# Thirteen small zero stores in place of two large ones, and new orders for four engines

## The chip, the cores and the metric

The kernel runs on one core of one Trainium2 chip. The metric is device time in microseconds (us). The kernel before takes 718.44 us, the median of three runs (717.93 to 718.69). Inside the core, TensorE (PE) multiplies matrices, VectorE (DVE), ScalarE (ACT) and GpSimd (POOL) work element by element, and SyncE (SP) issues most of the DMAs, one queue in order. The engines meet at semaphores.

## The reference, cut to what matters

A context of 16 batches of 1601 keys meets 64 queries a batch (width 256, 16 heads of 16), then the 64 rows attend to themselves, then each row goes to one of eight experts that has room for 128 rows.

```python
x = x + xattn(layernorm(x), ctx, ctx, Wq, bq, Wk, bk, Wv, bv, Wo, bo)   # x: 16 x 64 x 256, ctx: 16 x 1601 x 256
x = x + self_attn_with_rope(layernorm(x), Wqkv, bqkv, Wout, bout)
x = x + moe(layernorm(x), wg, W, b)

# moe: T = 1024 rows, E = 8 experts, C = 128 places each
idx = argmax(softmax(xt @ wg)); mask = one_hot(idx, E)
locations = cumsum(mask, axis=0) - mask
mask = mask * (locations < C)
exp_in  = einsum('tec,th->ech', dispatch, xt)
exp_out = einsum('ech,efh->ecf', exp_in, W) + b[:, None, :]
out     = einsum('tec,ecf->tf', gate * dispatch, exp_out)
```

## The kernel before, in words

**Cross attention, by batch.** A batch b passes through four kinds of work on PE. `project` (letter K in the order, L807 and L816) makes keys and values in float32 quality from three bf16 products. The units 0 to 7 of a batch are its keys, in two halves of four; 8 to 14 are its values. ACT rounds the result of each (`khigh`, L1213), DVE keeps the rest (`klow`, L1481). SP then copies the key rows of a half to `kstack`, 12 DMAs of 100 KB (`keys(b)`, L501), three for each pair of heads. `max_scores` (m, L839) multiplies queries with these keys to find each row's maximum, which DVE reduces (`maxes`, L1498). `score_half` (s, L867) makes scores again with the maximum taken off, ACT takes the exponent (`prob`, L1235), and POOL makes its low part (`plow`, L637; in part of the last batch DVE, L1468). `weigh` (w, L891) multiplies with the values.

**The second part** follows from letter Z on, in eight tiles of 128 rows: output projection, layer norm, self attention, routing, experts. For the first five tiles the rows are scattered to slots in DRAM (`slot_x`, L703), read back by expert (L534), multiplied, written to `slot_y` (L539) and gathered (L711). The last three tiles go through all experts (letter F). A row without a place lands in a spare slot, so the slots of `slot_x` and the spare slots of `slot_y` must hold zeros first.

**The zeros.** POOL clears `zeros` (L555, 128 rows of 256 floats), which is the last tile of `att_all`. DVE overwrites that tile only in `attended(14)` and `attended(15)`. SP sends the zeros to DRAM behind the DMAs of `keys(4)` (L516, L518), 1024 KB and 640 KB. POOL waits for both before the first scatter (L700).

**What sets the order.** Each engine runs a list of letters written out by hand: `PE_PROGRAM`, `ACT_PROGRAM`, `DVE_PROGRAM`, `POOL_PROGRAM`. A letter calls the next piece of its kind. SP has no such list: its loop runs `send_queries(0)` and then `keys(b)` for each batch. `keys(b)` waits until batch b-2 has been scored, reads the queries from DRAM (`qstack`, L494), copies the keys half by half as DVE finishes them, in even batches sends the next queries (L485), and waits until batch b is projected before it loads the context of batch b+2 (`cbuf`, L507, 1601 KB). All of this is one queue: a DMA issued later moves behind those before it.

In the lists of the second part, A is `attention_columns`, H `norm_columns`, J `queries_keys`, V `values`; on DVE p is `low_prob`, N `normalised`, L `first_low`, a `attended`, k `query_moments`, z `query_variance`, B `weight_parts(1)`, j `query_rows`; on POOL c is `low_context`, f `fold`, v `first_values_low`, q `query_norm`, r `inverse_root`, t `second_constant`, Z `rooms_empty`, b `first_constant`, I `low_experts`; on ACT g is `query_high`.

Of the kernel before, what the change touches and what calls it, by code (L numbers as in the profile page):

```python
# [107 lines left out]


PE_PROGRAM = [  # L110
    ("KKKKKKKKKKKKKmmKmmKmmKKmmKmKmKmmKmKmKmKmmKmKmmKmKmKmmKmKmmKmmsKmssmKsmmsKmsmswwsmswmKswsmmswwwKmswwm"
     "smsKKsmwKmsmswwmswswmwsmswmwwsmsmKmmsswwmwmKmwswwswwsKsmsKwwsmsKmsmsKsmmwswwmswmswmKmsswwmsKmmswKmsm"
     "wKmsmwwswmKwsmsmwKmwmKmswmsKmwssmwwKmKmwwsKswKwmssmKsmwsmsKsmwwwKmwwsmsmwswwmKmssmKmsmKmmswswmswmsKm"
     "smwwwswmmswKmsKmswsmwmKmsmsKwwwKwwsmwKsswKwsmKmsmsKmssKmwsKwwsmwmwKswwsmswmsKmwmKmswmKsmsmwwsKmsswmK"
     "wmwmswswmsmwwKmswmsKmmKmswmKwwmKwswsKwsKssKmmsKmsswwmKsswmmwKswwsmmswwsKmswsmwmKsmwwsmsmwmsKsmmKmwsw"
     "wmmsKwsmwswsmwKmmKmKmmwwwKwswmwKssKssKsmKmssmKwmwwsmwwmsKsmKwwsmwmKsmmKmmswKswwmssKmsmwwwsmsKmsmwKsw"
     "mmswsKmwmwssmKmmKmKwswwwwmwKwssKssmmKsmsmKwswsmmsKwmswsmKwmwwmswsKwssmmwKsmmKwsmswmwswwswmsmKwsmKmwm"
     "swKmsmKwmKmwKwswmmwKmsKssKmswmsKsmswmKssmwmwwsmwKsmKwswsmmwsKwmKswmsmKmswwswmwKmsswwmKsmsKwmwsswmmww"
     "KmsmKmmsKmmwwwwKswmwKssKssKswsmwmKmsswwmmKsmwKwmsswmwsKmsmswwmwmKsmsmKmswsmwmswKswmmswKsmKmmsKmswwms"
     "mwKmmKwwwwswmwKssKswsmmKsmwswsmwwmsKsmmsKmwmsswwKmswmKwswKsmmswKsswmwmwKmmKmsKwsmwsmwsmKswmKmwmKmmsK"  # L120
     "msKwwswwwmKssKswwsKmsmwKmssmwwmswwmswsmKmsKmwwwssmwmKmmsKssKmmwKmwsmwsmwsmKswmswmKmmssKmmKmwswmwswws"
     "KwwmwKssKwsswmmKsKmswswwsmwwsmsmKmswswwmKmwssKKKwwmssmwwsmKmmssmKwwwmmKsmswwmwssKmmsKmsmKmwmKmmwwwww"
     "swmKKssKKsmsmKssmmwswwsKsmKswwwmssmKmmwswwmwmwsKwmmsKsmmsKmwwsmwmsKmmssKmmKmwwmssmKmswwmwswwwKswmKsw"
     "wsKssKsmsmKsmsKmmwwsKwwsKmsmwwwmswmswsmKmwsmswmwwKsmKssmKwwmwsmwwmKmmssKsmmsKmwKwsmwmwKmmKwsmKsmswmw"
     "wsmsmKmsmKsKsmwmwswswwwsmmsKmKwmswsmwwmmssKmsmKsmwmwssmwwmswwsmmKsmswmswwsmmZmwswAswwwswsAwsOssOswws"
     "swwswswsswwsswwwssHwsHswwswwVssJswwswswTAJOTSVwwwwSPPwwHWVJP2APTOoWSAH2OJoPhPVTHlWVJS2AToOhSPPlhWlPA"
     "2POcHWoJ2AVOHToJHSVhThJllTcPVSPSWPP2Wo2PPoxhWlxgchxgxl2gogFcFhFFFFlFFcFFFF", 1),
]
ACT_PROGRAM = [
    ("KgKKKKKKKKKKKKKKKgKKKKKKKKKKKKKRRKeKeeeeKeeeKeeKeeKeKeeeKeeeeeeeKeeeKRReeKeKeeeeKeeeKeeKeeKeeKKeeege"  # L130
     "KKeeKeeKeReKRKKeeKeeeeKeKeeeKeeKeKeeeKeeKeeKeeeKeKReeKKReKeKeeKeeeKeKeKeKeeKeeKeKeeeKeeeegeeKeKKeRKR"
     "KeKeeeKKeeKeeKeeeeKeeeKeeeKeeKKeeeeeKeKKKRKeRKeeKeeeKKeeKeeeKKeKKeeeeKeeKeeegKeeeKeKeRKKeRKeeeKeeKee"
     "eKeeKeKeeKeeKeeeeKeeKKeeKKKKReeKReeKeKeeeKeeKeeeeKeeKKeeKeKeeKeeegKeeKeKeKRKReKeeeKeKeeKeeKeeKeeKeee"
     "eKeeKeeKKeeKeKeeKRKReKeeKeeeeeeKKeeKeeKeKeeKeeKKeKeegeKeKKeReKKeReKeeKeeeKeeKeeeKKeeKeeeKKeeKeeKeeKe"
     "KeKReKeReKeeKeeKeeeeKeeeKeKeKKeeeKeeeKKeegeeKKeeKKRKReKeeKeKeeeKeeKeeeeKeKKeeeKeKeeKeeKKeeKReeRKeeKe"
     "eKeKeeKeKeKeeeKeeeKeKeeKeeKeKeeKeKeKKReKReKeeeKeeKeeeeKeKeeeKeeKeeKeeZeeeeKeeRReAeeeeAeeeeeeeeeeeeee"
     "HeeeeHeeeTAVBTBVEEPPHVEEA2PTPBAH2EEPfPHBViTV2ABTEEfPPfEiEiAPlP2H2AHVBTHVffBiiETElTBPVPEEPP2EE2PPxfhi"
     "xyxflhyxi2lyyfhil", 1),
]
DVE_PROGRAM = [  # L140
    ("jKKkKKzCKKkBzKKmmkmmzkmmKmmjmmKmKmmKKKmmmKmmKmKmmKmKmKmmKmKmKmmKmmKmmmmKmmKmKKmmmmmmKmmmmmKmmmKvKmKm"
     "mammKmmmKmmKmmKmmmKmjmmKKmmmKmmmKmKmKKKKmmmvmKmKmmmmKmmKmKmmmmmmmKmKmmzmKmKmmKaKKKKmmmKmvKmKmmmkKmmm"
     "KKmmammKmmKmmjmmKmKmmmKKmKKKvKzmKmmmKmmKmmKmmKmmmmmKmKmmmKmmmKkamKmmKmKKKvKmKKmmmKmmmKmmmmKaKmmmKmmK"
     "mjmmKzmmmKmmKmKmKKvKmmKmmKmKmmmKKmammmKmKmmmKmmmKmmKmmKKmmKKmKKmmKmmvKmmKmmmmKmKmKmmaKmmKmjmmKmKmmmK"
     "mmKmKKKvKmKmmKmkmmKmamKmmKmmmmmKmKmmKmKmmzmKmmKmmKKKvmKmmmmKmmKmKmKmmmKmmKmmKmmKjmmKmamKmmKmKmKKKKvm"
     "mKmmmmKmmmKmKmKmmKmmKmmmmKammKmKmmmKmKKKKmvmKmmKmammKKmmKmmmKmmmKKmmjmmKmKmmmKmmKmKKKKmvmKmmaKKmmmmm"
     "KmKmmmKmmKmmmKmmKmmKmmmKKmKKKvmKmmKKmmmKmmKmmmKmmmKmKmmKmmKmmKmmKKmmmKaKmmKmmvmKmKmmamKmKmmmmmKmKmmm"
     "mmKmmmmKmZpvXDGXDGppNNpLapTLppTXDGMMUUMNULvMUWTXDxGdWgNMnLUXMUDxGTNdaLgWTnMMUxUdXgDMnMUUWG1NX3LDWxGN"
     "dTXDLGgxNdngLTnMMUUT13MMUUMWUMUWxdgnxdqg1nqWq31qxdgyn3yyyfyy1ffyy3yyffyy", 1),
]  # L150
POOL_PROGRAM = [
    ("qqvvcfcccvvffvvcccfcvfppppppcppppppppppppppcpccpppppcqppppcpppcppcppppccppppppcpqpppcpppcpppppppcppc"
     "pcpppppppcpcpqpcpppcpppccpppppcppppppcpccpppppppcpppppcppqpcpppppcppccpppppcppppcppppccpppppcpppppcp"
     "pcpqcpppppppppppcppppcccppppcpppppccpppcppppppcpcppppcpppcppppppppppppppppbbppprrpppZbbttbtbrrRIbrbR"
     "IRrtrtstsrRRIIsssttRYRYRgYgggg", 1),
]


# [1682 lines left out]
```

## Time and profile before

| what | value |
|---|---|
| three runs | 717.93, 718.44, 718.69 us |
| the profiled execution | 717.98 us, of which the span of the profile is 715.9 us |
| granted TensorE clock, mean | 0.988 |
| PE busy | 684.2 us, 96% |
| POOL, DVE, ACT busy | 78%, 77%, 62% |
| DMA | 84.20 MB, mean 118 GB/s |

The span is cut into stretches: for each, the busy time of every engine, the clock that PE was granted and what the DMAs moved. Where PE is busy the whole stretch at clock 1.00, only less PE work can make it shorter. A stretch in which PE is idle, or runs at half clock, is where another order or another transfer can matter. The profile also names, for each idle time, who ended it, and follows the chain of work that ended last back to the start.

### The profile page before, as it was taken

Reading aid. Unit: us, or ns where it says so; the run is one execution under the profiler, and the core shown is the slowest. Engines: PE = TensorE matmul, PEld = TensorE weight load, DVE = VectorE, ACT = ScalarE, POOL = GpSimd, SP = SyncE. Lnnn points to the kernel's source line nnn. Section 1 sums busy time; section 2 is a strip of 40 time slices with the busy share of each in tenths; the row PEclk is TensorE's granted clock in tenths of the full one; section 3 lists DMA queues with packets and bytes.
Section 4 is the critical chain, followed back from the end, with each engine's and each line's share of the span. In section 5 each row is a group of like instructions: output and inputs, shape, how many; then the busy total and the mean of one; then the engine's idle time right before and its main releaser. Section 6 shows DMA issues by size and latency. Waiting matters only on the chain.

```text
span 715.9 us, 21612 instructions
## 1 busy us (share of the span) xinstructions
PE 684.2 (96%) x8681; PEld 510.9 (71%) x8681; DVE 551.2 (77%) x1135; ACT 441.7 (62%) x884; POOL 558.0 (78%) x378
## 2 busy tenths in 40 slices
...
GB/s 313 129 218 201 32 121 164 95 153 92 234 79 145 105 154 99 142 88 173 91 158 90 165 91 158 90 164 84 160 99 111 101 145 2 1 3 16 77 65 96
DMA packets 45435, 84.20 MB, mean 118 GB/s; under 512 B 8493, under 2 KB 28245, under 8 KB 45333
## 3 DMA queue, kind: packets, MB, share of 16 engines
...
q8 instruction: 70, 1.15, 0.7%
...
## 4 chain that ended last, share of the span: by engine, by line
PE 82%; DVE 5%; POOL 4%; issue 3%; DMA 2%; ACT 2%; SPq 1%; POOLq 0%; ACTq 0%; DVEq 0%
PE ps_kv L816 17%; PE ps_kv L807 17%; PE ps_score L867 12%; PE ps_front L839 12%; PE ps_out L891 12%; DMA kstack<-khigh 2%; PE ps_score L915 2%; PE ps_front L915 2%; PE ps_kv L915 1%; DVE maxes L1498 1%; PE ps_front L848 1%; PE ps_out L907 1%; PE ps_kv L782 1%; POOL clow L579 1%; PE ps_out L816 1%
## 5 line engine op out<-in xcount | busy, mean ns | idle before, releaser
L637 POOL TENSOR_TENSOR plow<-prob 128x1024 bf16<-128x1024 f32 (+1 forms) x201 | 378.2, 1900 | 67.4 <-ACT prob L1235 64.1
L1498 DVE TENSOR_REDUCE maxes<-ps_front 128x1 f32<-128x512 f32 (+1 forms) x416 | 267.9, 666 | 58.7 <-PE ps_front L839 55.8
L1235 ACT ACTIVATE prob<-ps_score 128x512 f32<-128x512 f32 (+1 forms) x416 | 236.9, 598 | 88.0 <-PE ps_score L867 77.8
L867 PE MATMUL ps_score<-qstack,kstack 98*128 98x128 bf16 (+1 forms) x1664 | 153.2, 220 | 0.5 <-ACT prob L1235 0.2
L839 PE MATMUL ps_front<-kstack,qstack 96*128 96x512 bf16 (+1 forms) x512 | 146.6, 334 | 5.2 <-DMA kstack<-khigh 4.9
L867 PEld LDWEIGHTS ps_score<-qstack,kstack 98*128 98x128 bf16 (+1 forms) x1664 | 113.1, 99 | 30.6 <-ACT prob L1235 2.1
L891 PE MATMUL ps_out<-vstack,prob 128*128 128x65 bf16 (+1 forms) x1664 | 114.5, 194 | 2.8 <-DVE plow L1468 2.7
L1481 DVE SCALAR_TENSOR_TENSOR klow<-ps_kv,bcol,khigh 128x512 bf16<-128x512 f32 (+1 forms) x123 | 76.6, 629 | 47.6 <-ACT khigh L1213 47.2
L816 PE MATMUL ps_kv<-w_hi,cbuf 128*128 128x256 bf16 (+1 forms) x402 | 110.2, 274 | 0.3 <-DVE vstack L1488 0.3
L816 PE MATMUL ps_kv<-w_hi,clow 128*128 128x256 bf16 (+1 forms) x402 | 110.0, 274 | 0.0
L816 PE MATMUL ps_kv<-w_lo,cbuf 128*128 128x256 bf16 (+1 forms) x402 | 109.9, 273 | 0.0
L1213 ACT ACTIVATE khigh<-ps_kv,bcol 128x512 bf16<-128x512 f32 (+1 forms) x123 | 72.6, 593 | 58.5 <-PE ps_kv L807 57.1
L891 PEld LDWEIGHTS ps_out<-vstack,prob 128*128 128x128 bf16 (+1 forms) x1664 | 92.1, 98 | 19.7 <-DVE plow L1468 3.1
L579 POOL TENSOR_TENSOR clow<-cbuf 128x801 bf16<-128x801 f32 (+1 forms) x64 | 97.2, 1530 | 7.8 <-PE ps_kv L807 2.9
L891 PE MATMUL ps_out<-vstack,plow 128*128 128x33 bf16 (+1 forms) x1664 | 102.8, 178 | 0.0
L1221 ACT CAST vstack<-ps_kv 128x512 bf16<-128x512 f32 (+1 forms) x105 | 58.3, 555 | 48.8 <-PE ps_kv L816 48.5
L807 PE MATMUL ps_kv<-cbuf,w_hi 128*128 128x512 bf16 (+1 forms) x246 | 80.6, 341 | 1.6 <-DVE klow L1481 1.3
L807 PE MATMUL ps_kv<-cbuf,w_lo 128*128 128x512 bf16 (+1 forms) x246 | 80.6, 340 | 0.0
L807 PE MATMUL ps_kv<-clow,w_hi 128*128 128x512 bf16 (+1 forms) x246 | 78.8, 333 | 0.0
L891 PEld LDWEIGHTS ps_out<-vstack,plow 128*128 128x128 bf16 (+1 forms) x1664 | 75.0, 96 | 0.0
L1488 DVE TENSOR_TENSOR vstack<-ps_kv,vstack 128x512 bf16<-128x512 f32 (+1 forms) x105 | 67.8, 646 | 8.3 <-ACT vstack L1221 7.5
L839 PEld LDWEIGHTS ps_front<-kstack,qstack 96*128 96x128 bf16 x512 | 42.7, 97 | 17.3 <-issue 5.8
...
## 6 DMA issues: line engine op xcount, KB each, us to landing
kstack<-khigh SPq DMA_DIRECT2D x256, 100.1 KB, 2.2
cbuf<-in_ctxT SPq DMA_DIRECT2D x15, 1601.0 KB, 7.2
kstack<-klow SPq DMA_DIRECT2D x128, 100.1 KB, 2.2
...
q_blocks<-qbd SPq DMA_DIRECT2D x16, 128.0 KB, 2.0
...
```

The source lines that it names most:

```text
L579: nc.gpsimd.tensor_tensor(clow[par][:, k, a:a + n], cbuf[par][:, k, a:a + n], c_high(par, k, a, n), ALU.subtract).then_inc(clow_done, 1)
L637: nc.gpsimd.tensor_tensor(plow[slot][0:n, :], prob[slot][0:n, :], p_high(slot, 0, HP * P)[0:n], ALU.subtract).then_inc(plow_gps, 1)
L807: mm = nc.tensor.matmul(ps[:, 0:nn], w[0][:, k, t * P:(t + 1) * P], rhs, start=(j == 0), stop=(j == len(terms) - 1))
L816: mm = nc.tensor.matmul(ps[0:nn, a * D:(a + 1) * D], lhs, w[1][:, k, :], start=(j == 0), stop=(j == len(terms) - 1))
L839: mm = nc.tensor.matmul(ps[:, at:at + nn], qstack[par][0:96, q_at(hp), :], kstack[par][0:96, hp, n0:n0 + nn], start=True, stop=True)
L867: mm = nc.tensor.matmul(ps_score[0:nn, h % NSB, j * P:(j + 1) * P], kstack[par][0:98, hp, n0:n0 + nn], qstack[par][0:98, q_at(hp), :], sta ...
L891: mm = nc.tensor.matmul(o[:, 32 * part:OW], lhs, vstack[par][0:nn, k, hp, 32 * part:OW], start=(k == 0 and part == 0 and hp % 4 == 0), sto ...
L1213: nc.scalar.activation(khigh[:, t, n0:n0 + nn], kv_bank(b, u)[:, 0:nn], ACT.Identity, bias=bcol[:, 1, t:t + 1]).then_inc(high_done, 1)
L1235: nc.scalar.activation(prob[slot][0:nn, e * 512:e * 512 + 512], ps_score[0:nn, h % NSB, :], ACT.Exp)\
L1481: nc.vector.scalar_tensor_tensor(klow[:, t, n0:n0 + nn], kv_bank(b, u)[:, 0:nn], bcol[:, 1, t:t + 1], khigh[:, t, n0:n0 + nn], ALU.add, AL ...
L1488: nc.vector.tensor_tensor(v[:, :, :, 0:32], kv_bank(b, u)[0:rows, 0:nch * D].rearrange("p (c h d) -> p c h d", c=nch, h=HP), v[:, :, :, 32 ...
L1498: nc.vector.reduce_max(maxes[:, hp:hp + len(unit), n], ps[:, 0:len(unit) * nn].rearrange("p (h k) -> p h k", k=nn), AX.X).then_inc(m_free, 1)
```

## The change

The two large stores behind `keys(4)` go. In batches 1 to 13 SP sends one store of 128 KB behind `keys(b)`: eight fill the slots of `slot_x`, five the spare slots of `slot_y`. They land in the same bytes of DRAM as before. The semaphore counts that POOL waits for follow (208 in place of 32), and `attended(14)` waits on DVE until all thirteen stores have landed, since it writes over their source. The four lists of letters are new orders of the same letters: of 1674 letters on PE, 1077 positions differ, of 817 on ACT 355, of 872 on DVE 409, of 330 on POOL 125. No letter is added or dropped.

```diff
             send_queries(0)
             for b in BATCHES:
                 keys(b)
-                if b == SPOT_BATCH:
+                if 1 <= b <= E + BY_SLOT:
                     sp.wait_ge(zeros_set, 1)
-                    sp.dma_start(slot_x[0:SLOTS, :].rearrange("(e p) d -> p e d", p=P),
-                                 zeros.unsqueeze(1).to_broadcast([P, E, D])).then_inc(zeros_sent, 16)
-                    sp.dma_start(slot_y[SLOTS:SLOTS + BY_SLOT * P, :].rearrange("(e p) d -> p e d", p=P),
-                                 zeros.unsqueeze(1).to_broadcast([P, BY_SLOT, D])).then_inc(zeros_sent, 16)
+                    empty = slot_x[(b - 1) * P:b * P, :] if b <= E else slot_y[SLOTS + (b - 1 - E) * P:SLOTS + (b - E) * P, :]
+                    sp.dma_start(empty, zeros).then_inc(zeros_sent, 16)
...
             def rows_to_slots(t):
 
                 if t == 0:
-                    pool.wait_ge(zeros_sent, 32)
+                    pool.wait_ge(zeros_sent, 16 * (E + BY_SLOT))
...
             def attended(b):
 
                 dve.wait_ge(out_read, b + 1)
+                if b == B - 2:
+                    dve.wait_ge(zeros_sent, 16 * (E + BY_SLOT))
```

The lists differ from the first letters on. Their beginnings (PE has 36 letters in common and is not shown), and the letters around the start of the second part:

```diff
 DVE, start
-jKKkKKzCKKkBzKKmmkmmzkmmKmmjmm
+jkKBKzKCKkKKKzKkmmmmmmKmmjmmKm
 ACT, start
-KgKKKKKKKKKKKKKKKgKK
+KKgKKKKKKKKKKKKKKgKK
 POOL, start
-qqvvcfcccvvffvvcccfcvfppppppcppp
+qfccvvccfvvfvcqvvcccpppppcpppppp
 PE, from Z
-ZmswwAswwwswsAwsOssOswwsswwswswsswwsswwwssHwsHswwswwVssJswwswswTAJOTSV
+ZmswwAwsAswwswwsOssOswwsswwswswsswwswswwsswHswswHswsJswswsTJAVOTSV
 DVE, from Z
-ZpvXDGXDGppNNpLapTLppTXDGMMUUM
+ZpvXDGXDGppNpNaLpLTppTXDGMMUUN
 POOL, around Z
-ppbbppprrpppZbbttbtbrrRIbrbR
+pbbppprrtptpZbIprIbbrbbRtrbtR
```

## Rows read from the trace of the kernel before

**Rows 1.** The page: busy us of each engine (share of span) and instructions.
```profile
PE 684.2 (96%) x8681; PEld 510.9 (71%) x8681; DVE 551.2 (77%) x1135; ACT 441.7 (62%) x884; POOL 558.0 (78%) x378
```

**Rows 2.** The chain of work that ended last, two of its PE pieces.
```profile
186.86 0.22 PE ps_out L891 x8
...
187.21 1.34 PE ps_kv L807 x6
```

**Rows 3.** The same for the long middle after the zeros.
```profile
220.00:575.00 355.00, 352.64 (x4780) 268.11 (x4779) 280.22 (x541) 232.94 (x439) 301.07 (x173) 1.00 0.46 123
```

**Rows 4.** Stretches: length, busy us of PE, PEld, DVE, ACT, POOL, clock, DMA share, GB/s.
```profile
20.00:40.00 20.00, 17.20 (x120) 11.97 (x120) 13.37 (x30) 10.20 (x21) 15.29 (x15) 0.91 0.56 140
40.00:60.00 20.00, 18.61 (x140) 11.49 (x141) 17.55 (x35) 7.96 (x15) 17.73 (x18) 1.00 0.87 231
...
180.00:200.00 20.00, 16.44 (x190) 10.41 (x188) 12.01 (x27) 12.03 (x23) 13.05 (x8) 0.94 0.80 242
200.00:220.00 20.00, 20.00 (x267) 16.65 (x265) 14.22 (x27) 11.22 (x22) 15.85 (x9) 0.89 0.33 75
...
600.00:620.00 20.00, 18.40 (x240) 13.39 (x240) 13.55 (x22) 12.46 (x31) 12.35 (x18) 0.83 0.01 2
```

**Rows 5.** Timeline of PE around the stall: start us, us, instruction, [idle before <-releaser].
```profile
198.89 1.01 PE L839 MATMUL ps_front<-kstack,qstack 96*128 96x512 bf16 x2 [3.56 <-DMA kstack<-khigh]
```

**Rows 6.** Timeline of SP's DMA issues at batch 4: start us, us, instruction, count.
```profile
183.86 0.49 SPq L507 DMA_DIRECT2D cbuf<-in_ctxT  x1
...
184.92 2.48 SPq L518 DMA_DIRECT2D slot_y<-att_all  x1
187.50 4.44 SPq L494 DMA_DIRECT2D qstack<-q_blocks  x3
191.99 1.04 SPq L501 DMA_DIRECT2D kstack<-khigh  x1
```

**Rows 7.** Timeline of SP at batch 6, then at batch 12.
```profile
260.24 0.49 SPq L507 DMA_DIRECT2D cbuf<-in_ctxT  x1
...
267.69 0.52 SPq L501 DMA_DIRECT2D kstack<-khigh  x1
...
475.28 0.49 SPq L507 DMA_DIRECT2D cbuf<-in_ctxT  x1
476.43 1.58 SPq L494 DMA_DIRECT2D qstack<-q_blocks  x3
```

**Rows 8.** DMA issues: KB each, median us from issue to landing.
```profile
kstack<-khigh SPq DMA_DIRECT2D x256, 100.1 KB, 2.2
cbuf<-in_ctxT SPq DMA_DIRECT2D x15, 1601.0 KB, 7.2
...
q_blocks<-qbd SPq DMA_DIRECT2D x16, 128.0 KB, 2.0
```

**Rows 9.** Stretches of 1 us, where the clock fell and where it came back.
```profile
197.00:198.00 1.00, 0.00 (x0) 0.00 (x0) 0.00 (x0) 0.00 (x0) 0.25 (x1) 0.73 1.08 243
...
204.00:205.00 1.00, 1.00 (x22) 0.85 (x21) 0.07 (x2) 0.86 (x2) 0.06 (x1) 0.85 0.00 0
```

**Rows 10.** Timeline of DVE: the low part of the last key unit of the half.
```profile
190.25 0.29 DVE L1481 SCALAR_TENSOR_TENSOR klow<-ps_kv,bcol,khigh 128x65 bf16<-128x65 f32 x1 [0.20 <-ACT khigh L1213]
```

**Rows 11.** Timeline at the start: PE, then DVE, then ACT.
```profile
23.00 0.44 PE L772 MATMUL ps_kv<-cst,h 128*128 128x128 f32 x2 [2.80 <-POOL h L565]
...
21.89 0.93 DVE L1407 TENSOR_TENSOR w_lo<-att_all,w_hi 128x512 bf16<-128x512 f32 x1
```
```profile
12.81 0.84 ACT L1198 ACTIVATE qbd<-ps_kv,cst 128x256 bf16<-128x256 f32 x2 [3.71 <-DVE ps_kv L1426]
```

**Rows 12.** Timeline where the second part begins.
```profile
595.59 2.50 DVE L1570 TENSOR_SCALAR klow<-klow,mv,rs 128x256 f32<-128x256 f32 x2
...
598.01 2.91 DVE L1468 TENSOR_TENSOR plow<-prob 128x1024 bf16<-128x1024 f32 x1
...
600.98 0.40 PE L891 MATMUL ps_out<-vstack,prob 128*128 128x65 bf16 x4 [2.17 <-DVE plow L1468]
```

More of the change, by code:

```diff
@@ L110 @@
 PE_PROGRAM = [
[L111 to L127, printed above, removed]
@@ new lines @@
+    ("KKKKKKKKKKKKKmmKmmKmmKKmmKmKmKmmKmKmmKmKmmKKmmKmKmmKmKmmKmsKmmKmsmsKmsmsKmssmwwmwwssmKsmsmKsmwwwssmw"
+     "wmwsKsmKmssmKmmwwwsmswmwsmswmwsmsKmwswsmmKmwwswswwwswsKmmsswwKmsmswKKmsmswwmswwmwssmKmmKmmssKmswmwws"
+     "smKmwswwmwsmKswmwwmsKsmsKmmKmwsKwsmwmwKmKssKswmswmswwmKsmsmKwsmwmswKsmwwswmsmwKswmwmsKsmsmKmmwswswwm"
+     "wmsKmsswKmsmKmwswmswmKmmsKmswwKswwmwwKssKswsmmwsKmmsKsmmKwwsmwswmwwKwssmKKssmmwKmmswKmwsmwwsmswKmssm"
+     "KsmmwswwwmswmswwKmsmsKmKmmwKwsmwwwKwsKssKsKmsmKmswwsmmsKsmwwswmKmwwsswmKsmsmKwsmmwwwsswmmKsmmwwwssmK"
+     "smsKwmwmsKmsmKsmmKwmmwwwwwswKmwKssKsKsmmsKmmwwssmKmswswKwmswmwsKmKsswmmwsKwmswmKmsmsKmwmsKsmswwmsKmw"
+     "mswsKmwwmKssmmKmmwwwwKwwmswKsswKssmmKsmwmwssKsmwmsKmswwsmKwsmwKmmsKmsswKmswwmwwmwwsmswmwKmsKsmwmsKsm"
+     "mKmssmKmwwmwsKwwwsmKmKwssKssmmKwmswsKmmwsswwKmwsmwswKmsmKmswswwwmKmmsKswmmsKmwssmwKswsmwmwsKwmswmKsm"
+     "smKmmsKmmwwKwwwwsmwKssKswsmmKssmKmswwwswmwsmKKmssmwwwwmsmswKmsmsKmwsmswmKssmKmwwKsmmKmsmswwwmsmKmssw"
+     "mKmmwwwKwwwsmwKsswKssmKssmmKswsmwmwsKsmwmKswwmswwmKswsmwmKmswsmwKwmssmKmmsKmKswmswmwKwmwsmsKmKmsmKmm"
+     "wwwswwsKmwKsKsswKmwmssKsmmwswswmwwsmwKmwsmwKsmsKmsmKsmwsKmswwmmKmwwwmwsmsKsmwmsKsmsmKmsmKwmwswKmswmw"
+     "KsmwKswsKsmwwswmsmKsswmmwswswmKmmsswwwmwwmKKwssmKmwsmKssKmwsmKmwmsKsmwswmwKmsmwswKmsmsKsmwmKmmwwwwww"
+     "sKmwKsKssKsmsmKmsmwswwKmwsmswmwsKwmsmsKswmsmwwwwmssmKmwsmsKsmsmKmwmwwsKmsmKsmmKmKmssmwwmKwwwwswKmKww"
+     "ssmmKwmssmKsmsKswswwKmswmwwsmsKmswswwmwmsKsmmwwKmmssKmssmwwwwmsKsmswKmsmKKmsmwsKwwwmmwKmmKmwsKmwswsw"
+     "mmsKsmmsKmsswwmwsmwswKmwmssKmssmKmwmwsmKmsmwswwsmwmKmwmswswwmmssKmsmswwwsmmsZmswwAwsAswwswwsOssOswws"
+     "swwswswsswwswswswwsswHswswHswsJswswsTJAVOTSVwwwwwSPPwwHwWJVA2PTPOoWSA2HOoPJhPVlHWTJVAS2ThoOSPPhlWlP2"
+     "PAHocWOJAV2OHToJhSHlhTVlJVcPPTSWSPP2WoP2PxohWlxgchxg2lxgocgFhFFlFFFcFFFFFF", 1),
@@ L128 @@
 ]
 ACT_PROGRAM = [
[L130 to L138, printed above, removed]
+    ("KKgKKKKKKKKKKKKKKgKKKKKKKKKKKKRKeKRKeeeeKeeeKeeKeeKeeeKeKeeKeeeeeeeeRKReeeKeKeeKeeKKeeeKeeKeeKeeegee"
+     "KeeKeeKKKReeKRKeeeeKeeeKeKeeeKeKeeeeKeKeeKeeeKeKKeeRKKReeKeeeeKeKeeKKeeKeeKeKKeeeeeKKeeeegeeeKeKKRKR"
+     "eKeKeeKKeeeKeeKeeKeeKeeeKeeeeKeKeeKeKeKeKRKReKeeKeKeeeKeKeKeeKeeKeeeKKeKeeegeeKeeKKeeKRKReKeeKeeeKee"
+     "KeeKeKeKeeeeeKeeKKeKeeKeKeKeRKeeKRKeeKeeeKeKeeKeKeeeKeeKeKeKeeegeeeKKeKeeKRKReKeeKeeeeKeKeeKeKeeeeKe"
+     "eKeeKKKeeKeeeKeeKRKReKeeKeeeKeeKeeKeeKeKeeKeeKeKeKeegeeKeKeKKReeKRKeKeeKeeeeeeKKeeKeeKeKeKKeeeeKeKeK"
+     "eeKeKeRKReeKeeKeeeeeeKKeeKKeKeeKeKeKeeegeeeKeKeeKKRKeRKeKeeeKeeKeKeeeeeKKeeeeKeeKeKeeKKeeKKReKeeRKKe"
+     "eKeeeKeKeeeKeeeeKKeeKeeeKeeeKKeKeKKeeKRKeRKeeeeKeeeKeeKeeKeKeeeKeeZKeeeeKeeeeRReAeeAeeeeeeeeeeeeeeee"
+     "HeeHeeeeeBATVBTVEEPPHEEVAPT2PBAH2EPEfPHVTiBAV2BTfEEPPfiEEiP2PHlAA2VHBTfHifBiEElTVPPBVTEEPP2EE2PPxfhi"
+     "xlyxhfy2ixyyhflil", 1),
```

26 lines of the change are left out of this document (13 added, 13 removed).

## The prediction

> **What bounds the kernel now.** I read the page's busy times first. PE is busy 96% of the span [rows 1]; the span is 715.9 us, so PE is idle for 715.9 − 684.2 = 31.7 us. The chain of work that ended last is PE almost throughout. Its pieces run at the pace of the array: six key products of 512 columns in 1.34 us, eight small products in 0.22 us [rows 2]. So the stretches come next, to see where PE's 31.7 us and its lost clock lie. From 220 to 575 us PE is idle for only 355.00 − 352.64 = 2.4 us [rows 3]: there only less PE work would help, and the change takes no PE work away. What can be won lies in three places [rows 4]: 180 to 220 us (PE idle 3.56 us, clock 0.94 and 0.89), the start (20 to 40 us: idle 2.8 us, clock 0.91), and the beginning of the second part (600 to 620 us: idle 1.6 us, clock 0.83).
>
> **The stall at 195 us and the two stores.** PE's largest wait in the middle is one of 3.56 us, for the key copies: the first maxima of batch 5 start at 198.89 us, and PE had been done since 195.3 us [rows 5]. SP's timeline just before shows the two stores behind a context load [rows 6]. The issue of the second takes 2.48 us, the three query loads behind it 4.44 us in place of the 1.58 at batch 12 [rows 7], the first key copy 1.04 us in place of 0.52. The bytes agree with this. One context load moves 1601 KB in 7.2 us [rows 8], 222 KB a us. Load and stores are 1601 + 1024 + 640 = 3265 KB, or 14.7 us; from 183.86 us that ends at 198.6 us, where PE's wait ends. Key copies wait behind this backlog instead of landing in 2.2 us.
>
> The idle time also cost clock. The granted clock fell from 2.4 to 1.2 GHz at about 197.5 us and came back at about 204.3 us (the clock means of these two single microseconds are 0.73 and 0.85) [rows 9]. PE worked from 198.9 to 204.3 us at half pace: 5.4 / 2 = 2.7 us lost. Together 3.56 + 2.7 = **6.2 us**.
>
> **What goes when the stores are small.** Without the large stores, the three query loads start at 187.50 and take 1.58 us. The last low part of the half ends at 190.5 us [rows 10], the third copy starts two issues of 0.52 us [rows 7] later and lands after 2.2 us: near 193.8 us, ahead of PE, which came at 195.3. So I take the whole 6.2 us as gained. What is late next is this same hand-over, with about 1.5 us to spare.
>
> **What the thirteen small stores add.** Each is 128 KB. A DMA of that size (`q_blocks`) lands in 2.0 us [rows 8], and issuing a DMA of 128 rows takes 0.5 us (0.49 for the context load [rows 6]). Its time on the wires is 128 / 222 = 0.58 us. It is sent right behind the context load. Behind it on SP's queue stand the query loads and then the key copies of the next batch, for which PE waits. The tightest place is batch 12, where the query loads follow 1.15 us after the context load's issue began, so 0.66 us after it ended [rows 7]: one issue fits. For the bytes, at batch 6 the first key copy comes 267.69 − 260.24 = 7.45 us after the context load [rows 7], while load and store together take 7.2 + 0.58 = 7.8 us: the copies may land some 0.3 us later, in batches that have this spacing. In the new PE list I counted the work between the last key product of the first half and the first maximum, with 1.34 us a full key product, 1.31 us a value product and 0.22 us a piece of s, w or m. From batch 3 on it is 4.7 to 6.9 us before and 4.9 to 6.6 us after. The key copies need, at batch 5, 190.54 − 189.44 = 1.1 us from the end of the last product to the end of its low part [rows 10], 1.0 us for two issues and 2.2 us to land: 4.3 us. So at least 4.9 − 4.3 = 0.6 us is left. Lower bound 0 (all hidden), upper bound 13 x (0.5 + 0.58) = 14 us (nothing hidden); I take **+0.3 us**, because the rows lie near the hidden end.
>
> The Trainium skill ("DMA: Bandwidth & Descriptors", the table of what to do) speaks against this edit: many small transfers should be made into one large one. Its section on the anatomy of one DMA gives each about 2.0 us of fixed cost; by it the eleven extra DMAs would be 22 us if they stood on the path. The 2.0 us landing of `q_blocks` agrees with that page. No row here has anything wait for a zero store.
>
> **The added waits.** `attended(14)` on DVE waits for the thirteenth store, which leaves behind `keys(13)`. The piece runs while PE weighs batch 15, more than a batch later, and a batch takes some 35 us ((575 − 220) / 10). Behind it on DVE would stand L and p, for which PE waits; but it waits for nothing. SP's wait for `zeros_set` now stands at batch 1, and clearing the tile is POOL's fourth instruction. POOL's first scatter comes in the second part. All at nothing.
>
> **The new orders, start.** DVE does B before the first keys' low parts, ACT takes the first key copy before g. So `query_low(0)` ends later by my estimate of 2 us (a first key copy that must be made, and then g, stand before it), then comes B (its second part alone 0.93 us [rows 11]), and the fifth key product waits for its bank some 1.1 us. This comes out of the 2.80 us in which PE waits for POOL's h anyway [rows 11], since POOL reaches it only behind its ten DMA issues, which stay. PE's idle time splits into 1.1 and 1.8 us. If the clock then doesn't fall, up to 0.09 x 20 = 1.8 us is gained. POOL moves context low parts into a gap and finishes the last v earlier, which may give back part of the 20.00 − 18.61 = 1.4 us idle between 40 and 60 us [rows 4]. Bounds −3.2 and +1 us (a value part that comes late); I take **−0.8 us**, half the clock.
>
> **The new orders, middle.** Counted over batches 2 to 14, the smallest distance in PE work between a score and the one that uses its bank again goes from 0.89 to 1.08 us; from a maximum to the next in its bank 0.67 to 0.89; from a score to its w 2.98 to 3.28. A little more room everywhere. Bounds −2.4 us (all idle time of [rows 3]) and +3 us (a few new waits of 0.7 us); I take **−0.4 us**.
>
> **The new orders, second part.** PE waits 2.17 us for DVE's p of chunk 6, which runs behind two N [rows 12], and the clock after it costs 0.17 x 20 = 3.4 us in the stretch from 600 to 620 us [rows 4]. The new list has p between the two N, 1.2 us sooner. But PE also gets there sooner, since the second H and two more s now come behind; the wait is about as long. On POOL, t comes between the last p, and Z, b and I before p of chunk 9, which PE needs only after J, T, J, A, V, O, T, S, V. Bounds −6 us (wait and clock gone) and +5 us (another wait of 2.2 us, with its clock); I take **−0.5 us**.
>
> **Sum.** −6.2 + 0.3 − 0.8 − 0.4 − 0.5 = −7.6 us. Against the profiled execution, 717.98 − 7.6 = 710.4 us. That execution is 0.46 us under the median of the three runs, so 710.8 us is forecast for the median.
>
> **The rivals.**
> - *The small stores reach the key copies.* If the copies of each batch have less than their 1.08 us to spare, the delay comes back thirteen times: 13 x 1.08 − 7.9 = +6.1 us, so 724.5 us. It is slower than before from 7.9 / 13 = 0.6 us a batch on. For it: the hand-over has 0.6 us by my count, less than 1.08, and batch 12 leaves no more than 0.66 us on SP. Against it: in the middle PE is idle for 2.4 us in 355.
> - *The stall isn't the stores'.* SP also waited for PE's scores until 187.5 us, so the hand-over of batch 5 could stay late for another reason. Then only the small terms are left: 718.44 − 1.4 = 717.0 us, up to no change. Against it: the bytes, and that no other batch has such a stall.
> - *The second part gets better too.* Its clock no longer falls: 710.8 − 5 = 705.8 us.
> - *The second part gets worse.* One more wait of 2.2 us and 3.4 us of clock: 716.4 us. For it: POOL's p of chunk 9 now stands behind 5 us of other work.
>
> **How the numbers follow.** Forecast 0.54, small stores exposed 0.10, stall stays 0.07, second part better 0.13, worse 0.16. This kernel can tell about 0.2% from no change, 1.4 us. Faster by more: 0.54 + 0.13 + 0.16 + 0.03 of the stall rival = 0.86; within: 0.04; slower: 0.10. The range runs from 705.5 to 716.8 us, and leaves out the exposed stores and most of the staying stall; the order terms alone, with their bounds, make it that wide.
>
> **What the profile after would show.** Stores right: no wait over 1 us of L839 at batch 5, clock 1.00 from 180 to 220 us, three query loads in about 1.5 us there, and SP's new DMAs each 0.5 us. Exposed stores would show as waits of L839 for `kstack` in many batches. Start: the clock from 20 to 40 us above 0.91, and PE waiting for h. Second part: the idle time before w of chunk 6 and the clock from 600 to 620 us. I am wrong if the middle, now 2.4 us of idle time in 355, holds many small waits, which no count of distances excludes, or if the clock falls at a new place.

## The result, and the profile after

The changed kernel takes 710.5 us (median of four runs, 709.23 to 711.0), the kernel before 718.18 us beside it. The ratio is 0.9891, with a 95% interval of 0.9874 to 0.9908. The forecast was 710.8 us. The profiled execution took 709.23 us; its span is 707.1 us, 8.8 us less than before. The term for the stall held. The terms for the new orders did not: a gain ahead of the second part and a loss in it partly cancel.

In the trace after, lines 519 to 1528 stand two lower: the maxima are L837, the weighing L889, DVE's `plow` L1466, POOL's L635 and L679, the small stores L517. It lacks 45 matmul records (8636 of 8681), so a little of PE's idle time is only a missing record. The rest of the page answers [rows 1] and [rows 8]:

```profile
PE 673.3 (95%) x8636; PEld 508.9 (72%) x8681; DVE 556.5 (79%) x1135; ACT 443.4 (63%) x884; POOL 555.8 (79%) x378
...
kstack<-khigh SPq DMA_DIRECT2D x256, 100.1 KB, 2.2
cbuf<-in_ctxT SPq DMA_DIRECT2D x15, 1601.0 KB, 6.8
...
slot_x<-att_all SPq DMA_DIRECT2D x8, 128.0 KB, 6.6
```

The key copies land in 2.2 us as before. A small store needs 6.6 us behind a context load, and nobody waits for it. The stretches that answer [rows 4], with the same columns, the two at the beginning of the second part in halves:

```profile
20.00:40.00 20.00, 17.09 (x125) 11.90 (x125) 13.10 (x28) 10.46 (x21) 18.07 (x19) 1.00 0.60 150
...
180.00:200.00 20.00, 19.87 (x246) 14.03 (x245) 14.76 (x29) 14.13 (x28) 17.69 (x12) 1.00 0.61 176
...
580.00:590.00 10.00, 6.51 (x145) 5.31 (x142) 9.35 (x10) 6.75 (x13) 10.00 (x8) 0.97 0.01 2
590.00:600.00 10.00, 6.40 (x58) 4.90 (x60) 7.50 (x6) 3.13 (x6) 8.90 (x14) 0.52 0.01 2
```

From 180 to 200 us PE is busy for 19.87 us at clock 1.00, where it was 16.44 at 0.94. The bad place is now 580 to 600 us: PE is idle for 7.1 us, and the clock is 0.52 in the second half, nearly all of it at 1.2 GHz. SP's issues at batch 4, which answer [rows 6], and PE's two waits that tell of the start and of the second part:

```profile
182.99 0.49 SPq L507 DMA_DIRECT2D cbuf<-in_ctxT  x1
183.52 0.49 SPq L517 DMA_DIRECT2D slot_x<-att_all  x1
184.11 1.61 SPq L494 DMA_DIRECT2D qstack<-q_blocks  x3
189.85 0.52 SPq L501 DMA_DIRECT2D kstack<-khigh  x1
```
```profile
28.98 0.59 PE L837 MATMUL ps_front<-kstack,qstack 96*128 96x512 bf16 x2 [1.06 <-DMA kstack<-khigh]
...
593.38 0.40 PE L889 MATMUL ps_out<-vstack,prob 128*128 128x65 bf16 x4 [5.02 <-DVE plow L1466]
```

**Where the 8.8 us are.** The loads of the context (L507) are marks that both traces have. At batch 4 the mark stands at 183.86 us before and 182.99 after, one batch later at 222.37 and 214.54. The first matmul of letter Z (L907, after L905) starts at 581.95 and 572.37 us, the spans end at 715.9 and 707.1. The distance thus grows to 0.87 us up to batch 4, by 6.96 us in the batch with the stall, by 1.75 us up to Z, and shrinks by 0.78 us in the second part.

### The profile page after: what moved, and what is told of

The parts are those of the page before. It is cut to its first block, busy times and chain, and to the rows that moved or that the text cites. A ratio compares the mean times of both kernels' runs of the same rounds, so it can differ in the third digit from the quotient of the medians.

```text
span 707.1 us, 21580 instructions
## 1 busy us (share of the span) xinstructions
PE 673.3 (95%) x8636; PEld 508.9 (72%) x8681; DVE 556.5 (79%) x1135; ACT 443.4 (63%) x884; POOL 555.8 (79%) x378
## 4 chain that ended last, share of the span: by engine, by line
PE 82%; DVE 6%; DMA 5%; issue 3%; SPq 2%; ACT 1%; POOL 0%; ACTq 0%; DVEq 0%; POOLq 0%
PE ps_kv L814 17%; PE ps_kv L805 16%; PE ps_score L865 12%; PE ps_front L837 12%; PE ps_out L889 11%; DMA kstack<-khigh 3%; SPq L501 2%; PE ps_score L913 2%; PE ps_kv L913 2%; PE ps_front L913 1%; PE ps_kv L780 1%; DVE maxes L1496 1%; DMA wq_sb<-in_wqT 1%; PE ps_out L905 1%; DMA q_blocks<-qbd 1%
## 5 line engine op out<-in xcount | busy, mean ns | idle before, releaser
L635 POOL TENSOR_TENSOR plow<-prob 128x1024 bf16<-128x1024 f32 (+1 forms) x201 | 377.1, 1892 | 57.0 <-ACT prob L1233 50.0
L837 PE MATMUL ps_front<-kstack,qstack 96*128 96x512 bf16 (+1 forms) x512 | 146.1, 333 | 4.5 <-DMA kstack<-khigh 3.9
L889 PE MATMUL ps_out<-vstack,prob 128*128 128x65 bf16 (+1 forms) x1664 | 114.0, 194 | 6.6 <-DVE plow L1466 5.8
L889 PEld LDWEIGHTS ps_out<-vstack,prob 128*128 128x128 bf16 (+1 forms) x1664 | 91.8, 98 | 24.1 <-DVE plow L1466 6.3
L889 PE MATMUL ps_out<-vstack,plow 128*128 128x33 bf16 (+1 forms) x1664 | 102.5, 178 | 0.0
L889 PEld LDWEIGHTS ps_out<-vstack,plow 128*128 128x128 bf16 (+1 forms) x1664 | 74.9, 96 | 0.0
L805 PE MATMUL ps_kv<-cbuf,w_hi 128*128 128x512 bf16 (+1 forms) x212 | 67.2, 332 | 0.4 <-DVE klow L1479 0.4
L837 PEld LDWEIGHTS ps_front<-kstack,qstack 96*128 96x128 bf16 x512 | 42.9, 97 | 13.2 <-issue 4.6
```

The lines of the kernel that those rows point to most:

```text
L635: nc.gpsimd.tensor_tensor(plow[slot][0:n, :], prob[slot][0:n, :], p_high(slot, 0, HP * P)[0:n], ALU.subtract).then_inc(plow_gps, 1)
L805: mm = nc.tensor.matmul(ps[:, 0:nn], w[0][:, k, t * P:(t + 1) * P], rhs, start=(j == 0), stop=(j == len(terms) - 1))
L837: mm = nc.tensor.matmul(ps[:, at:at + nn], qstack[par][0:96, q_at(hp), :], kstack[par][0:96, hp, n0:n0 + nn], start=True, stop=True)
L889: mm = nc.tensor.matmul(o[:, 32 * part:OW], lhs, vstack[par][0:nn, k, hp, 32 * part:OW], start=(k == 0 and part == 0 and hp % 4 == 0), sto ...
```

## The experiments

The theory after the result: the stores cost some 6 us; the orders give 1 to 2 us before Z and nothing behind it, where they leave a loss that another order can remove. The rivals: it was the orders that removed the stall; small stores cost something in every batch; the wait in the second part has another cause than the place of the work on POOL.

### One part without the other

The changed kernel again, on the chip of the next three variants:

> The changed kernel again, beside the variants of it on one chip. Both theories expect 710.5 us within 1 us, 7.7 us under the kernel before.

709.5 us, ratio 0.9877 (0.9856 to 0.9898). The kernel before took 718.32 us there. Here all records are in the trace, and the wait at the beginning of the second part is again 5.0 us.

The old orders with the small stores (of the change, only the part on SP and the counts):

```diff
-PE_PROGRAM, ACT_PROGRAM, DVE_PROGRAM, POOL_PROGRAM = new orders
+PE_PROGRAM, ACT_PROGRAM, DVE_PROGRAM, POOL_PROGRAM = orders of the kernel before
```

> The four orders of before, with the thirteen small stores. Theory (the two large stores made the stall at 195 us, the small ones cost nothing): 718.2 - 6.2 = 712.0 us, no wait over 1 us for the key copies at batch 5 and clock 1.00 from 180 to 220 us. Rival (the new orders made the gain, the stall was a tight hand-over of the old order): 717 to 718 us, with the 3.6 us wait still there. Rival (small stores reach the key copies): several waits for key copies of about 1 us, above 714 us.

711.14 us, ratio 0.99 (0.9878 to 0.9922).

The new orders with the two large stores behind `keys(4)`:

```diff
-                if 1 <= b <= E + BY_SLOT:
+                if b == SPOT_BATCH:
                     sp.wait_ge(zeros_set, 1)
-                    sp.dma_start(empty, zeros).then_inc(zeros_sent, 16)
+                    (the two stores of the kernel before)
```

> The new orders, with the two large stores behind the keys of batch 4. Theory: the stall comes back whatever the order, since its length is that of the backlog of 3265 KB: 710.5 + 6.2 = 716.7 us, a wait of 3 to 4.5 us for key copies near 195 us and half clock after it. Rival (the reserve of the new orders covers it): 710.5 to 712 us.

715.52 us, ratio 0.9954 (0.9933 to 0.9976). The stall is back whatever the order. Its timeline on SP, then on PE:

```profile
184.88 2.33 SPq L518 DMA_DIRECT2D slot_y<-att_all  x1
187.31 4.64 SPq L494 DMA_DIRECT2D qstack<-q_blocks  x3
191.99 0.90 SPq L501 DMA_DIRECT2D kstack<-khigh  x1
```
```profile
198.97 0.38 PE L839 MATMUL ps_front<-kstack,qstack 96*128 96x512 bf16 x1 [4.10 <-DMA kstack<-khigh]
```

These are close to the durations of [rows 6] and the wait of [rows 5]. The medians make a square. With the old orders the small stores bring 718.32 − 711.14 = 7.2 us, with the new ones 715.52 − 709.5 = 6.0 us. The orders bring 1.6 us with small stores, 2.8 us with large ones. Each ratio is known to about 0.2%, or 1.5 us, so neither the 7.2 and the 6.0 nor the 1.6 and the 2.8 can be told apart. The marks say it more sharply: from the load of batch 4 to that of batch 5 the two kernels with large stores need 38.51 us (old orders) and 37.46 us (new ones), those with small stores 32.32 and 31.55 us. Old orders: 6.2 us; new orders: 5.9 us. The rival that the orders removed the stall falls.

What the orders bring shows at letter Z. It starts at 581.95 us (large stores, old orders), 579.87 us (large, new), 574.81 us (small, old) and 572.70 us (small, new): the new orders bring 2.1 us with either kind of store, and the small stores 7.1 and 7.2 us. The two kernels with small stores up to Z, with the columns of [rows 4], old orders and then new ones (a record that only reaches into a stretch is counted too):

```profile
0.00:574.81 574.81, 558.79 (x7357) 421.07 (x7357) 448.25 (x873) 367.40 (x696) 496.68 (x313) 1.00 0.50 135
0.00:572.70 572.70, 556.60 (x7356) 419.98 (x7357) 450.16 (x872) 368.83 (x695) 496.18 (x312) 1.00 0.50 135
```

PE is idle for 16.0 and 16.1 us, at clock 1.00 in both, and the same letters stand ahead of Z. So these 2.1 us are not waits: the same matmuls, in the new order, keep PE busy for 2.2 us less. Why they do is not shown.

### How many stores

Two large stores out of the way, behind `keys(15)`, with the new orders:

```diff
-                if 1 <= b <= E + BY_SLOT:
+                if b == B - 1:
                     sp.wait_ge(zeros_set, 1)
-                    sp.dma_start(empty, zeros).then_inc(zeros_sent, 16)
+                    (the two stores of the kernel before)
```

> The new orders, the two large stores sent behind the keys of the last batch, where no key copy follows. It takes the small stores out of the batches and so prices them. Theory (small stores nearly hidden, 0.3 us): 710.2 us. Rival (the six waits of the profile after for key copies, 3.9 us together, come from the small stores): 707 us, and these waits at 1.5 us or less together.

710.0 us, ratio 0.9881 (0.9859 to 0.9902), against 709.5 us with thirteen small ones on the same chip. PE waits for key copies 2.7 us in 5 waits there, 3.9 us in 7 with small stores. So thirteen small stores cost some 1.2 us of waits in a trace (with them Z also starts 1.4 us later, at 572.70 against 571.34 us), and nothing that the medians show.

Four stores, in between:

```diff
-                if 1 <= b <= E + BY_SLOT:
+                if b in ZERO_STORES:     # {3: (0, 0, 4), 6: (0, 4, 4), 9: (1, E, 3), 12: (1, E + 3, 2)}
                     sp.wait_ge(zeros_set, 1)
-                    sp.dma_start(empty, zeros).then_inc(zeros_sent, 16)
+                    into, first, count = ZERO_STORES[b]
+                    sp.dma_start((slot_x, slot_y)[into][first * P:(first + count) * P, :].rearrange("(e p) d -> p e d", p=P),
+                                 zeros.unsqueeze(1).to_broadcast([P, count, D])).then_inc(zeros_sent, 16)
```

> The new orders with the same zeros in four stores, behind the keys of batches 3, 6, 9 and 12 (512, 512, 384, 256 KB) in place of thirteen of 128 KB. If the delay of the key copies goes by bytes on the wires (222 KB a us in the trace of before), a store of 512 KB puts them 2.3 us later, where the small one puts them 0.6 us later and the waits for them are at most 1.1 us: waits of PE for the key copies of 1.5 to 3 us at the batches behind 3 and 6, none that is new behind 12, and clock falling at one or two of them: 711.5 to 714. If instead only a backlog like that of the two large stores on one batch (1664 KB) matters, 709.5 to 710.5, with no new wait over 1.1 us.

710.54 us, ratio 0.9907 (0.9885 to 0.9929). The whole trace has four waits for key copies, the longest 1.0 us (here, as in the kernels with large stores, the maxima are L839 again):

```profile
PE ps_front L839 <- DMA kstack<-khigh: 2.6, 4, 1.0
```

The store of 512 KB at batch 6 makes the first key copies behind it land in 2.5 to 3.0 us, where they take 2.1 to 2.2 us behind one of 128 KB, and PE sees nothing of it; 1664 KB in one batch cost 6 us. The rival that each byte sent pushes the copies back until PE waits is too strict: the copies have slack that takes in 512 KB. Where between 512 and 1664 KB the slack ends was not tried.

### The second part

New orders up to the scores of the last batch, the old ones behind them:

```diff
-lists from there on: new orders
+lists from there on: orders of the kernel before
```

> Small stores; the new orders up to the start of batch 15's scores, then the old orders for the rest on all four engines. In the profile after, PE waits 5.0 us for p of chunk 6 and then works 6 us at half clock, while the old order had a wait of 2.2 us there. Theory (the new second part loses there and wins about as much back later): 709.5 - 0.8 = 708.7 us, with a wait of about 2.2 us for p of chunk 6. Rival (the new second part is better by what my prediction took, 0.5 us, or more): 710 to 712 us.

710.19 us, ratio 0.988 (0.9852 to 0.9908). The old end is no better behind the new beginning; 708.7 us had been expected. PE waits elsewhere, 3.42 us for the first N:

```profile
590.79 0.69 PE L899 MATMUL ps_kv<-cst,klow 128*128 128x128 f32 x2 [3.42 <-DVE klow L1570]
```

DVE's p of chunk 6 ahead of both N:

```diff
-DVE ...DGppNpNaLpLT...
+DVE ...DGpppNNaLpLT...
```

> The changed kernel with one edit on DVE: p of chunk 6 before both N. In the profile after, N took 2.66 us ahead of it. Theory: PE's wait before w of chunk 6 falls from 5.0 to about 2.4 us, then H waits for N; 707 to 708.5 us. Rival (N and the wait are slow because POOL works on the same memory at that time, whatever the order on DVE): no gain, 709.5 us.

710.91 us, ratio 0.9887 (0.9856 to 0.9917): no gain. PE's wait for p falls from 5.0 to 2.4 us as the theory said, but a wait of 3.5 us for N follows it. POOL's two t behind Z:

```diff
-POOL ...bbppprrtptpZbIp...
+POOL ...bbppprrppZttbIp...
```

> The changed kernel with one edit on POOL: both t move behind p of chunk 8 and Z. Theory (DVE's N and p are slow since POOL runs t and p beside them): N ends about 1.5 us sooner and the wait of 5.0 us falls to about 3.5 us; 708 us. Rival (DVE's pieces take what they take): the wait stays at 5 us and the time at 709.5 us.

**704.3 us**, ratio 0.9798 (0.9771 to 0.9826), against 710.2 and 710.9 us for the two kernels before it on the same chip. It gives some 6 us, the wait and its clock:

```profile
580.00:590.00 10.00, 8.30 (x173) 6.84 (x171) 9.29 (x13) 7.86 (x16) 10.00 (x6) 1.00 0.01 2
590.00:600.00 10.00, 9.54 (x106) 6.68 (x104) 8.61 (x14) 7.69 (x20) 9.57 (x15) 1.00 0.01 2
```

From Z to the end it needs 701.8 − 572.89 = 128.9 us, the changed kernel 134.7, the kernel before 133.95. Both edits together, and PE's first two H behind Z four and two letters later:

```diff
-PE ...sswHswswHswsJ...
+PE ...sswswswHswHsJ...
```

> The changed kernel with p of chunk 6 before both N, both t later, and on PE the first H behind w of chunk 7. Theory (the wait for p is the cause of the half clock): the longest wait is 2.4 us or less, PE has 2.7 us less idle time and the clock keeps 2.4 GHz from 590 to 600 us; 704.5 us, ahead of both kernels. Rival: the wait only moves to H, 709 us.

707.03 us, ratio 0.9837 (0.9809 to 0.9864): worse than the one edit alone by 2.7 us, clock 0.91 from 580 to 600 us. On DVE the two N, now behind p, are late:

```profile
582.64 5.74 DVE L1466 TENSOR_TENSOR plow<-prob 128x1024 bf16<-128x1024 f32 x3 [0.50 <-ACT prob L1233]
588.30 3.88 DVE L1570 TENSOR_SCALAR klow<-klow,mv,rs 128x256 f32<-128x256 f32 x2
```

The second ends at 592.18 us, in the kernel of 704.3 us at 590.59. But PE waits for neither N. Its longest wait in these 20 us is for ACT, before a score (letter s), and the half clock follows it:

```profile
591.81 0.61 PE L865 MATMUL ps_score<-qstack,kstack 98*128 98x128 bf16 x4 [0.96 <-ACT prob L1233]
...
592.00:596.00 4.00, 4.00 (x30) 2.47 (x29) 2.95 (x7) 1.60 (x4) 3.57 (x12) 0.63 0.02 6
```

With the H moved back, more s come before the first H. That points at H's place rather than p's; the two added edits were not run apart, so it stays open.

**Why t matters.** DVE and POOL stand in each other's way. DVE around the wait, in the changed kernel, and POOL beside it:

```profile
587.15 2.66 DVE L1570 TENSOR_SCALAR klow<-klow,mv,rs 128x256 f32<-128x256 f32 x1
589.73 3.59 DVE L1466 TENSOR_TENSOR plow<-prob 128x1024 bf16<-128x1024 f32 x1
```
```profile
586.46 1.35 POOL L679 TENSOR_TENSOR vstack<-klow,khigh 128x256 f32<-128x256 f32 x1
587.77 1.89 POOL L635 TENSOR_TENSOR plow<-prob 128x1024 bf16<-128x1024 f32 x1
589.62 0.76 POOL L679 TENSOR_TENSOR vstack<-klow,khigh 128x256 f32<-128x256 f32 x1
590.35 1.88 POOL L635 TENSOR_TENSOR plow<-prob 128x1024 bf16<-128x1024 f32 x1
```

With nothing of POOL beside it, this p takes 1.21 us on DVE (at 601.26 us in the same trace). Here it starts at 589.73 us, while POOL is in a t, and another p of POOL follows at once. It ends at 589.73 + 3.59 = 593.32 us, that is 1.09 us after POOL's p (590.35 + 1.88 = 592.23). So DVE did its work only when POOL's had ended. N ends at 589.81 us, 0.15 us after POOL's p before (589.66), and is 2.66 us long in place of 0.40. The kernel with p first shows the same arithmetic, DVE and then POOL:

```profile
588.36 3.59 DVE L1466 TENSOR_TENSOR plow<-prob 128x1024 bf16<-128x1024 f32 x1
```
```profile
588.98 1.89 POOL L635 TENSOR_TENSOR plow<-prob 128x1024 bf16<-128x1024 f32 x1
```

588.36 + 3.59 = 591.95 us, 1.08 us after 588.98 + 1.89 = 590.87. That is why calling p earlier on DVE gave nothing: p took 3.59 us there too, and now the first N behind it was held, for 4.13 us. With t behind Z:

```profile
587.15 0.40 DVE L1570 TENSOR_SCALAR klow<-klow,mv,rs 128x256 f32<-128x256 f32 x1
587.47 1.21 DVE L1466 TENSOR_TENSOR plow<-prob 128x1024 bf16<-128x1024 f32 x1
```
```profile
586.48 1.15 POOL L685 TENSOR_TENSOR rs<-ve,half_neg 128x1 f32<-128x1 f32 x1
587.60 2.83 POOL L635 TENSOR_TENSOR plow<-prob 128x1024 bf16<-128x1024 f32 x1
```

N comes while POOL is in r, takes 0.40 us all the same, and it is r that is long: 1.15 us, where the same r takes 0.54 us in the changed kernel (at 585.95 us). DVE's p starts 0.13 us ahead of POOL's, takes 1.21 us, and now POOL's p is the longer one, 2.83 us. It ends at 590.43 us, 1.75 us after DVE's (588.68). The p for which PE waits is done 588.68 − 572.89 = 15.8 us after Z, where it was 593.32 − 572.37 = 21.0 us in the changed kernel and 600.92 − 581.95 = 19.0 us before [rows 12]. The 5.2 us between the first two are DVE's long instructions: 2.26 us on N, 2.38 us on this p and 0.53 us on the p ahead of N (1.74 us against 1.21).

That t stands behind Z is not enough by itself. It does so in the kernel before, where the second N took 1.98 us and p 2.91, and in the kernel with the old end, where the first N, begun 0.67 us after the same r as in the kernel of 704.3 us, took 4.34 us beside two p of POOL. So the same distance from r ended in two ways, and what decides between them no run shows.

The Trainium skill ("SBUF — State Buffer", the section on SBUF's two separate sides) describes such a thing: DVE and GpSimd share one pair of ports as an exclusive lock, held for a whole instruction, and the one that comes later is fully blocked; it holds for a DVE instruction in a two-port mode, or for one with two inputs in SBUF against a GpSimd instruction that reads SBUF. The ends 1.08 and 1.09 us behind POOL's, and the 2.83 us in the other direction, agree with that page. The N of 0.40 us that came while POOL was in r does not follow from it. What the runs show is the order of the ends; that it is a port no trace says. Of the 6 us, the 5.2 us by which p comes sooner are held instructions; how much of the rest is the clock, and how much that POOL's last two p no longer have a t ahead of them, is not separated.

### The start, and the best of both

The kernel of 704.3 us with the old beginnings:

```diff
-ACT KKgKK...   DVE jkKBKzKCKkKKKzKk...   POOL qfccvvccfvvfvcqv...
+ACT KgKKK...   DVE jKKkKKzCKKkBzKKm...   POOL qqvvcfcccvvffvvc...
```

> The kernel that gave 704.3 with the beginnings of the lists as before the change: ACT's first 19 letters, DVE's first 20, POOL's first 16; PE's first 36 are the same in both anyway. If the start is worth what the first context load's move shows (44.40 to 43.14 us), 705.4 to 705.8, with PE waiting about 2.8 us in one piece for POOL's h and a clock near 0.91 from 20 to 40 us. If the start gives nothing and the 1.3 us come from elsewhere, 704.0 to 704.6.

704.0 us, ratio 0.9809 (0.9784 to 0.9834). The wait for h is one piece of 2.80 us again and the clock is 0.91 from 20 to 40 us, but the time is not longer:

```profile
22.31 0.69 PE L770 MATMUL ps_kv<-cst,h 128*128 128x128 f32 x2 [2.80 <-POOL h L563]
...
20.00:40.00 20.00, 17.40 (x120) 12.29 (x123) 13.00 (x26) 10.02 (x21) 15.41 (x14) 0.91 0.56 145
```

Its first context load of SP stands at 43.53 us, against 43.04 us with the new start. In these traces the gain is given back at the first maxima: with the new start PE arrives sooner and waits there for the key copies, 1.29 us in the kernel of 704.3 us and 1.06 us in the changed kernel (the row at 28.98 us above); with the old start there is no such wait. The difference is small beside the scatter: over the ten traces with the new start this load stands anywhere from 42.51 to 43.48 us, over the three with the old one at 42.96, 43.53 and 44.40 us.

The same kernel with the new start and the two large stores behind `keys(15)`, the two edits shown above together:

> The new orders with POOL's two t moved behind Z (the edit that gave 704.3), and the zeros in two large stores behind the keys of the last batch in place of thirteen small ones. If the small stores are free where they stand, 704.0 to 704.8, as between the same two placements with the new orders unedited (709.5 and 710.0). If the small waits for key copies (0.6 to 1.3 us, six of them) come from the small stores, 702 to 703.5 and the waits fall to half.

704.2 us, ratio 0.9809 (0.9784 to 0.9834). Again small stores and late large ones can't be told apart. The waits for key copies are 2.5 us in 5 here and 4.9 us in 6 with small stores, yet the medians are 704.2 and 704.3 us. The two traces show where it goes: with late stores Z starts 1.4 us sooner (571.54 against 572.89 us), and from Z to the end it takes 130.5 us against 128.9. Whether the late stores cause the second part of that is not shown.

## Why the prediction was right, and where it was not

**What bounds the kernel.** Right for the stall, which is most of the gain, and for the second part. Wrong in the sentence that from 220 to 575 us "only less PE work would help", which left nothing for an order to win: the new orders bring 2.1 us up to Z with PE's idle time unchanged, since the same matmuls keep PE busy for 2.2 us less.

**The stall, −6.2 us.** Right in size and cause. The square gives 7.2 and 6.0 us by medians, 6.2 and 5.9 us by the marks. The key copies are issued from 189.85 us on, each in 0.52 to 0.6 us, where it was 191.99 us and 1.04 us for the first, and PE has no wait over 1 us there. One agreement came by chance: the bytes gave 198.6 us as the end of the backlog, but the second large store had landed 11.5 us after its issue, at 196.4 us. What reached to PE's 198.9 us were the copies themselves, issued late and landing in 3.6 to 5.0 us in place of 2.2. (3.56 + 2.7 is 6.26, so the term is nearer 6.3.)

**The small stores, +0.3 us.** Right within the measurement: the medians show nothing by the comparison with late large stores, the traces up to 1.4 us at Z. They issue in 0.47 to 0.49 us, one of them in 0.94. The row that misled a little is the landing of 2.0 us taken from `q_blocks`: it is 6.6 us here, since they stand behind a context load. It cost nothing because no engine waits for it. What matters here is how much stands in the queue ahead of a transfer that is awaited. The Trainium skill ("DMA: Bandwidth & Descriptors", the table of what to do and the anatomy of one DMA) asks for few large transfers, and its 2.0 us of fixed cost, given there for DMAs that GpSimd issues, would make an estimate of 22 us for eleven more on the path. No such cost appears: these come from SP and are off the path.

**The start, −0.8 us.** The split came as told: the wait for h went from 2.80 to 1.74 us with pieces ahead of it, and the clock stayed at 1.00. The worth did not follow. The traces show 0.5 us, within their scatter, and the medians nothing (704.0 against 704.3 us). The step that failed is "If the clock then doesn't fall, up to 0.09 x 20 = 1.8 us is gained": it asked what the clock costs, not what comes next. Next came the first key copies. Nor is the clock tied to the split: with the old orders and small stores PE waited for h 2.62 us in one piece and the clock did not fall:

```profile
20.00:40.00 20.00, 17.38 (x132) 12.20 (x131) 15.35 (x33) 10.46 (x21) 16.80 (x16) 1.00 0.62 152
```

**The middle, −0.4 us.** Too small. By the marks the new orders bring 0.8 us between the loads of batches 4 and 5 (32.32 against 31.55 us), and 0.97 us from there to Z with the small stores (359.09 against 358.12 us). The idle time of PE did not fall: from 220 to 560 us it is 1.6 us before and 2.5 us in the full record of the changed kernel. So my bound of −2.4 us, all idle time, measured the wrong thing: the failed step is that an order can only win idle time. No work was moved behind Z either, since both lists have the same letters ahead of it. Start and middle together bring 2.1 us up to Z, where −0.8 − 0.4 = −1.2 us was taken, and it is PE's busy time that falls.

**The second part, −0.5 us.** Wrong, and in sign: +0.8 us, or +2.3 us between the two kernels with small stores (132.5 us from Z to the end with the old orders, 134.8 with the new ones). I wrote that p now stands between the two N and so comes 1.2 us sooner. It came 21.0 us after Z in place of 19.0. The failed step is the price of p and N. I took the order of the letters on DVE and moved one duration. But [rows 12] show 2.50 us for two N and 2.91 us for p, where 0.40 for one N and 1.21 are their own times; those long rows were waits for POOL, and the change moved two t of POOL right beside them. The sentence "on POOL, t comes between the last p" stood there, and drew no cost on DVE from it. The clock fell with the wait, to 0.52 from 590 to 600 us. It does not follow every wait, though. The old orders with small stores had the 2.17 us wait, and clock 1.00 from 560 to 620 us:

```profile
593.83 0.30 PE L889 MATMUL ps_out<-vstack,prob 128*128 128x65 bf16 x4 [2.17 <-DVE plow L1466]
...
560.00:620.00 60.00, 54.18 (x826) 43.64 (x824) 47.60 (x86) 42.59 (x97) 42.54 (x38) 1.00 0.21 58
```

**The sum** came within 0.3 us because the errors cancel: by the traces −0.87 up to batch 4, −6.96 in the stall's batch, −1.75 up to Z, +0.78 behind it, against −6.2 + 0.3 − 0.8 − 0.4 − 0.5. **The rivals.** "The small stores reach the key copies" fell with the late and the four stores, "the stall isn't the stores'" with the square. "The second part gets better" and "worse" both exist as kernels: 704.3 us is the one, and the changed kernel stands a little on the side of the other.
